# Setup joined to the batch loop, with the first two batches' head-0 scores taken from small fp32 products

## The reference

```python
x = L0_attn_x                                  # (B=8, T=512, C=128)
xn = layernorm(x)
x = x + attn(xn) + ffn(xn)

# attn: 16 heads of 8; q, k, v = split(xn @ w_attn.T + b_attn)
att = q @ k.T / sqrt(8), causal
S = relu(att[:, 0]); S[..., 0] = 0; S[diagonal] = 0
FF = cumsum(S shifted down by one row, axis=1)
att = att - FF[:, None]                        # for all 16 heads
keep = rank of FF in its row < min(101, i + 1), or the diagonal
y = softmax(where(keep, att, -inf)) @ v
attn = y @ w_proj.T + b_proj

# ffn: gates softmax(xn @ gate_w.T + gate_b), top 2 of 8 experts
inter_e = xn @ wi.T + bi + (xn @ lora_A[e].T) @ lora_B[e].T
ffn = sum over chosen e of (top_1 + top_2) * (relu(inter_e) @ wo.T + bo)
```

## Time and profile before

| | |
|---|---|
| median of 3 runs | 795.98 us (793.61 to 798.28) |
| the profiled execution | 799.05 us |
| its span, first to last instruction | 797.1 us |
| mean granted TensorE clock | 0.933 |
| busy: TensorE, VectorE, ScalarE, GpSimd | 592.1, 549.3, 378.2, 435.4 us |

### The profile page before, as it was taken

The page is one execution under the profiler, slowest core; times in us unless marked ns, Lnnn a source line. Parts: engine busy times, 40 slices in busy tenths (PEclk is TensorE's granted clock), DMA queues, the critical chain, the costliest instruction groups (busy, mean ns, idle before and its releaser), DMA issues. The chain is left out here.

```text
span 797.1 us, 16830 instructions
## 1 busy us (share of the span) xinstructions
PE 592.1 (74%) x5478; PEld 400.7 (50%) x5478; DVE 549.3 (69%) x2257; ACT 378.2 (47%) x806; POOL 435.4 (55%) x739
## 2 busy tenths in 40 slices
PE   4233029888788888878987878878888788879995
PEld 2111026465555564556645654547546664656574
DVE  6746416599748984699669964798459864897352
ACT  4124105564546554564556454645455454635443
POOL 4322226546845584547754684557564684439542
PEclk9998559999999999999999999998999899989998
DMA  3511130002500051003200250005100240000000
GB/s 83 66 14 25 26 53 5 1 2 38 71 1 2 14 72 23 1 1 58 50 1 1 36 73 1 2 1 71 23 2 2 43 53 1 1 11 6 1 2 14
DMA packets 27287, 18.98 MB, mean 24 GB/s; under 512 B 5418, under 2 KB 27073, under 8 KB 27201
## 3 DMA queue, kind: packets, MB, share of 16 engines
q1 hardware_dynamic: 27200, 17.91, 15.2%
HBM read 3.22 MB, written 2.10 MB: 7 GB/s over the span
## 5 line engine op out<-in xcount | busy, mean ns | idle before, releaser
L506 POOL TENSOR_SCALAR ar<-ar,mx 128x512 f32<-128x512 f32 (+3 forms) x512 | 280.2, 559 | 242.8 <-DVE mx L1156 242.0
L1156 DVE CUSTOM_DVE_ANT_0 ar<-ps_s,mask 128x512 f32<-128x512 f32 (+3 forms) x512 | 231.1, 485 | 77.3 <-PE ps_s L798 74.5
L809 PE MATMUL ps_t<-ident,ar 128*128 128x128 f32 x1280 | 210.0, 284 | 40.4 <-ACT pr L657 24.2
L657 ACT ACTIVATE pr<-ps_t 128x512 f32<-128x512 f32 (+1 forms) x352 | 191.0, 554 | 95.5 <-PE ps_t L809 94.9
L809 PEld LDWEIGHTS ps_t<-ident,ar 128*128 128x128 f32 x1280 | 158.3, 145 | 82.9 <-POOL ar L506 63.4
L798 PE MATMUL ps_s<-ks,qs 96*128 96x512 bf16 (+3 forms) x512 | 133.2, 314 | 41.6 <-PEq L1195 38.1
L825 PE MATMUL ps_o<-pr,va 128*32 128x128 f32 x2560 | 103.3, 292 | 18.9 <-ACT out_t L666 11.3
L798 PEld LDWEIGHTS ps_s<-ks,qs 96*128 96x128 bf16 x512 | 44.3, 102 | 92.2 <-issue 69.8
L825 PEld LDWEIGHTS ps_o<-pr,va 128*32 128x32 f32 x2560 | 66.4, 114 | 47.2 <-ACT pr L657 29.5
L642 ACT ACTIVATE h<-ps_m,bi_col 128x512 f32<-128x512 f32 x64 | 43.8, 685 | 83.4 <-PE ps_m L756 83.4
L756 PE MATMUL ps_m<-zm,b_t 128*128 128x512 f32 x128 | 70.0, 629 | 5.7 <-ACT h L642 5.4
(11 more groups left out here) (172 smaller groups left out, 801.9 us busy)
## 6 DMA issues: line engine op xcount, KB each, us to landing
qs<-parts SPq DMA_DIRECT2D x48, 128.0 KB
ks<-parts SPq DMA_DIRECT2D x48, 128.0 KB
xs<-in_L_attn_x SPq DMA_DIRECT2D x8, 256.0 KB, 3.3
out<-res SPq DMA_DIRECT2D x8, 192.0 KB, 2.1
out<-res SPq DMA_DIRECT2D x8, 64.0 KB, 6.4
ar<-in_L_ffn_wi SPq DMA_DIRECT2D x1, 256.0 KB
ar<-in_L_ffn_wo SPq DMA_DIRECT2D x1, 256.0 KB
ar<-in_L_ffn_lora_B SPq DMA_DIRECT2D x4, 64.0 KB
```

The lines of the kernel that those rows point to most:

```text
L506: nc.gpsimd.tensor_scalar(col, col, -1.0, mx[:, t % NA_RING, j:j + 1], ALU.mult, ALU.add)\
L657: nc.scalar.activation(pr[:, u % NP_RING, 0:w], ps_t[u % NT_RING][:, 0:w], ACT.Exp, scale=-1.0)\
L809: last = nc.tensor.transpose(ps_t[u % NT_RING][:, P * j:P * j + P], ar[:, u % NA_RING, P * j:P * j + P], ident[:, :])
L1156: nc.vector.tensor_tensor_reduce(out=ar[:, t % NA_RING, w * j:w * j + w], in0=ps_s[t % NS_RING][:, w * j:w * j + w], in1=mask[:, k % 2, OF ...
```

## The change

The two blocks become one. The slots of the setup are numbered from -26 (`AHEAD`) to -1 and run straight into slot 0.

- SP issues x, the attention weights, the eight small weights, the second x, and then the large feed-forward weights. Each job waits for its own weights.
- In the setup the side jobs rotate over all eight PSUM banks.
- Batch 0's and batch 1's head-0 scores no longer read the stacks. Two fp32 products of depth 128 with 8 output rows (`q0`, `k0`) give q and k of head 0 alone, and `s0` to `s3` are fp32 products of depth 8 from these (`head0`, which borrows the tiles `res` and `down`). Other batches take the stacks as before.
- Batch 1's moments, norm and transposed input stay in the setup; its q, k, parts, stacks and routing move into the first slots of batch 0 (`SECOND_AT`).
- The memsets of stack 0 are now one ahead of the moments and one behind them on VectorE; those of stack 1 come right behind the first root on GpSimd. `bqk_dh` is made by ScalarE.
- The split of the output biases (`bias_parts`) runs on VectorE at slot 9 of batch 0, and its transfer is waited for by GpSimd's first sum of hidden layers (`w_rows`).
- For all later batches scores, scans, reads and search of head 0 start two slots later (`s0` 13 to 15, `scan0` 14 to 16, `f0` 18 to 20, `search` 22 to 24, `under` 30 to 32, `reach` 31 to 33), while `marks` and what follows stay. `z` moves from slot 1 to 5, `mask0` and `mask1` from 3 and 4 to 7 and 8.
- x has three buffers instead of four, `ar` seven slots instead of six.

```diff
-XN = 4
+XN = 3
-NA_RING, NP_RING = 6, 6
+NA_RING, NP_RING = 7, 6
-FFN_JOBS = [("z", 1, "act"), ("mask0", 3, "dve"), ("mask1", 4, "dve")] + \
+FFN_JOBS = [("z", 5, "act"), ("mask0", 7, "dve"), ("mask1", 8, "dve")] + \
...
+AHEAD = 26
+FIRST_AT = {
+    "moments": 0, "root": 0, "norm": 1, "xt": 2, "q": 9, "k": 9,
+    "rest_q": 9, "second_q": 10, "third_q": 13, "rest_k": 9, "second_k": 11, "third_k": 13,
+    "s0": 5, "s1": 6, "s2": 7, "s3": 8, "scan0": 6, "scan1": 7, "scan2": 8, "scan3": 9,
+    "f0": 9, "f1": 10, "f2": 11, "f3": 12,
+    "gate": 14, "route": 16, "choices": 21, "share": 24,
+    "search": 13,
...
+    "flag": 24, "mask_0": 24, "mask_1": 24, "mask_2": 24, "mask_3": 24, "v": 25,
+}
+SECOND_AT = {
+    "moments": 3 - AHEAD, "root": 3 - AHEAD, "norm": 21 - AHEAD, "xt": 22 - AHEAD, "q": -1, "k": 0,
+    "rest_q": 0, "second_q": 1, "third_q": 2, "rest_k": 1, "second_k": 2, "third_k": 3,
+    "gate": 2, "route": 4, "choices": 6, "share": 7,
+}
...
+HEAD_JOBS = [("q0", 0, 3 - AHEAD), ("k0", 0, 3 - AHEAD), ("q0", 1, 23 - AHEAD), ("k0", 1, 23 - AHEAD)]
+WEIGHT_JOBS = [("w_attn", 0), ("small", 9), ("rows", 9), ("w_in", 20), ("w_out", 20), ("lora_b", 20)]
+BIAS_AT = 9
...
+        head0 = [tile[0:HD, :, :].rearrange("d a c -> d (a c)") for tile in (res, down)]
...
+                        elif name in ("q0", "k0"):
+                            wait_read(pe, "xt", n)
+                            wait_read(pe, "w_attn", 0)
+                            heads = (wq if name == "q0" else wk)[:, :].rearrange("c (d h) -> c d h", d=HD)
+                            last = nc.tensor.matmul(m[0:HD, :], heads[:, :, 0], xnt[:, c, :], start=True, stop=True)
...
                             j = int(name[1])
-                            if nth(n) >= 0:
-                                pe.wait_ge(stacked, 192 * (nth(n) + 1))
+                            if n <= 1:
+                                wait_read(pe, "k0", n)
+                                last = nc.tensor.matmul(m[:, 0:T - P * j], head0[1][:, P * j:P * j + P],
+                                                        head0[0][:, P * j:T], start=True, stop=True)
+                            else:
+                                pe.wait_ge(stacked, 192 * (n + 1))
...
+                                    if f == 0:
+                                        if k >= 1:
+                                            wait_full(pool, "down1", k - 1)
+                                        else:
+                                            pool.wait_ge(w_rows, 32)
...
-                    for t in range(end):
+                    for t in range(-AHEAD, end):
...
-        run_block(0, 1, setup=True)
-        run_block(STEPS, STEPS - 1)
+        run_block()
```

More of the change, by code:

```diff
@@ L112, with __init__ @@
     [(f"s{c}", "act") for c in range(NA)] + [(f"f{a}", "dve") for a in range(NA)] + [("flag", "dve")]
[L114 to L119, removed]
+NW, NW_SMALL = 6, 8
+HEAD_JOBS = [("q0", 0, 3 - AHEAD), ("k0", 0, 3 - AHEAD), ("q0", 1, 23 - AHEAD), ("k0", 1, 23 - AHEAD)]
+WEIGHT_JOBS = [("w_attn", 0), ("small", 9), ("rows", 9), ("w_in", 20), ("w_out", 20), ("lora_b", 20)]
+BIAS_AT = 9
 class Plan:
[L125 to L130, removed]
+    def __init__(self):
+        jobs = [(o - AHEAD, (name, 0), "act") for name, o in WEIGHT_JOBS]
+        jobs += [(t, (name, m), "act") for name, m, t in HEAD_JOBS]
+        for k in range(B):
             jobs += [(NU * k + o, (name, k), who) for name, o, who in FFN_JOBS + ATT_JOBS]
-        jobs += [(self.slot(name, n), (name, n), who) for name, who in PREP_JOBS
-                 for n in (self.early if name in EARLY else self.late)]
+        jobs += [(self.slot(name, m), (name, m), who) for name, who in PREP_JOBS for m in range(B)]
         jobs.sort(key=lambda x: x[0])
-        self.at, self.number, self.place, self.reads, self.last = {}, {}, {}, {}, []
+        self.at, self.number, self.bank, self.before, self.reads = {}, {}, {}, {}, {}
+        self.last = {}
         counts = {"act": 0, "dve": 0}
+        early, now, pair = 0, 1, None
         for i, (t, key, who) in enumerate(jobs):
@@ L140, in __init__, with slot @@
             if key[0][0] == "h" and key[0][2] == "1":
-                self.place[key] = self.place[key[0][:2] + "0", key[1]]
-                self.last[self.place[key]] = key
-            else:
-                self.place[key] = len(self.last)
-                self.last.append(key)
+                bank, pair = self.bank[key[0][:2] + "0", key[1]], None
+            elif pair is not None:
+                bank = 1 - pair
+            elif t < 0:
+                bank, early = early % NBANKS, early + 1
+            else:
+                bank = 1 - now
+            if t >= 0:
+                now = bank
+            if key[0][0] == "h" and key[0][2] == "0":
+                pair = bank
+            self.bank[key] = bank
+            self.before[key] = self.last.get(bank)
+            self.last[bank] = key
+            if bank >= NM_RING:
+                assert t < 0
             counts[who] += 1
             self.reads[key] = (who, counts[who])
[L150 to L156, removed]
+    def slot(self, name, m):
+        if m == 0:
+            return FIRST_AT[name] - AHEAD
+        if m == 1 and name in SECOND_AT:
+            return SECOND_AT[name]
+        return PREP_AT[name] + NU * (m - 1)
 def build(nc, x, w_attn, b_attn, w_proj, b_proj, wi, bi, wo, bo, lora_a, lora_b, gate_w, gate_b, out):
@@ L386, in make_stacks @@
                             stack, part = ((qs, Q_PART), (ks, K_PART))[t]
                             for j in range(len(part)):
-                                sp.dma_start(stack[8 * j:8 * j + 8, into(n), :, :], parts[:, t, part[j], :])\
-                                    .then_inc(stacked, 16)
-                    fetch(1)
-                    if setup:
-                        make_stacks(0)
-                        sp.wait_ge(w_prep, 3)
-                        for j in range(2):
-                            sp.dma_start(bias_rows[0:3, j, :, :], bias_part[:, j, :, :, :]).then_inc(w_rows, 16)
-                        sp.wait_ge(w_rows, 32)
@@ L398, in _ @@
-                    for k in range(steps):
-                        if k in plan.early:
-                            make_stacks(k)
+                                sp.dma_start(stack[8 * j:8 * j + 8, into(m), :, :],
+                                             parts[:, t, part[j], :]).then_inc(stacked, 16)
+                    fetch(0)
+                    sp.dma_start(raw_attn, w_attn.rearrange("(t p) c -> p t c", p=P)).then_inc(w_first, 16)
+                    sp.dma_start(raw_bqk[:, :], b_attn[0:2 * P].rearrange("(t p) -> t p", p=P)).then_inc(w_first, 16)
@@ L445, in pool_prepares @@
                     def pool_prepares(n, t):
-                        if setup and n == 0 and t == at("third_k", 0) + 1:
+                        if n == 1 and t == at("root", 0):
                             for stack in (qs, ks):
@@ L658, in _ @@
                                 .then_inc(weighed, 1)
-                        for kk in range(steps):
+                        for kk in range(B):
                             for a in range(NA):
@@ L785, in fill, with wait_early @@
                         last.then_inc(m_full, 1)
+                    def wait_early(bank):
+                        for i, one in enumerate(banks):
+                            if one is bank and i in plan.last:
+                                wait_read(pe, *plan.last[i])
                     def score(u):
```

380 lines of the change are left out of this document (201 added, 179 removed), and 8 rows, old and new, of tables (FIRST_AT, PREP_AT).

## The result

The kernel with the change took 750.46 us, the median of 4 runs (746.2 to 753.04), against 796.45 for the kernel before (4 runs, 793.61 to 798.28): a ratio of 0.9422 with a 95% interval of 0.9381 to 0.9462. The forecast was 750.6. The profiled execution took 753.04 with a span of 751.2, 45.9 less than the span of before.

A forecast was written before the change was run, and what follows sets the result against it. Bound: a long setup (first loop score at 114.04 us), then TensorE and VectorE by turns within batches. Lead 42.9 after batch 0 plus 2.5 later makes 45.4, off 799.05 profiled: 753.7, or 750.6 for the median; range 736 to 765.

The forecast's parts named there:

- The front of the setup: Setup up to the loop's first score: without stacks for head 0, that score comes at 60.2 instead of 114.04, 53.8 us earlier.
- What comes back in batch 0: Batch 0: GpSimd, late until 75.1, cuts the lead to 47.4 us; another 4.5 behind it leaves 42.9.
- the split biases: VectorE at slot 9 of batch 0: 3.5 to 7.2 us there, 0 to 5 on the path, 1.9 taken.
- the price of the later search: Stretch between search start and its unchanged end slot: VectorE's loses two units, TensorE's gains two, +1.8 us per batch, seven batches.
- the eight such waits: Slot 9 of batch 0: VectorE's bias split waits for GpSimd shifts of some 0.46 us, adding at most 3.7 us.
- The rows' wait: GpSimd's first sum, slot 16 of batch 0, waits for the bias rows' transfer: 0.5 us taken, bounds 0 and 6.
- the late bound: Upper bound of 6 us for the bias rows' wait; called the likely landing if rows queue behind the stack transfers.
- Later batches: Loop after batch 0: 5.3 us of stack waits saved, 2.8 lost net over seven batches, so 2.5 less in all.
- z's move: Later batches: z and its two masked products leave VectorE's full stretch for slots 5 to 8, -1.4 us per batch.
- Nothing comes back: Rival, chance 0.14: the lead of 53.8 us stays through batch 0 and later batches give 8, so 734 us.
- The long setup: Rival, chance 0.22: GpSimd's memsets lengthen the setup by 7.0 us or batch 0 loses 5.5 more: 763.1, up to 778.
- The exact selection: Rival, chance 0.02: a row's count leaves its bounds, thirteen exact rounds run once, 52 us more: 802.6 us.

The follow-up runs named there:

- bias_setup: Changed kernel with the split of the output biases made in the setup, ahead of the first scan, instead of at slot 9 of batch 0: 747.77 us, ratio 0.939.
- z_early_rows: Changed kernel with early z and masked products after batch 0, biases split in the setup, bias rows issued between both batches' stacks: 738.02 us, ratio 0.93.
- both_old: Changed kernel with both slot moves undone for later batches (head-0 scores to search, and z with its masked products): 758.13 us, ratio 0.9525.
- z_early: Changed kernel with z back at slot 1 and its masked products at 3 and 4 in batches 1 to 7: 743.29 us, ratio 0.9335.
- stacks0: Changed kernel with batch 0's head-0 scores waiting for the stacks again and 34 setup slots instead of 26: 777.55 us, ratio 0.975.
- large_first: Changed kernel with the large weights' loads issued ahead of the small ones again, as in the kernel before: 747.2 us, ratio 0.9414.

## Why the forecast was right, and where only its sum was

*The front of the setup: right.* The four small products took 4.6 us from 16.0, where 5.1 were summed; the search began 2.1 earlier than forecast (30.2 against 32.3), and the last mask was complete at 62.3, not 63.7. The first score came 0.8 later than forecast (60.97 against 60.2), and this closeness is partly luck: the stacks were issued 2.1 us earlier than forecast (31.35 against 33.5) and took 29.6 us from issue to first use and not 26.7, longer than the 27 that the prediction names as a sign of being wrong. The stack alone set the first score: the first mask was there 2.7 us earlier, at 58.3. The fp32 row was the one to take for the small products in this execution; in others they took 2.4 us in all, nearer to the bf16 bound of 1.5 (last section).

*What comes back in batch 0: GpSimd right in its end, the rest short by 3.6.* GpSimd came free at 75.0 as summed, but it began its shifts 1.4 us earlier than forecast and waited 0.48 and 1.16 us for VectorE between them, where the prediction had no gap. Its lead was then 47.5 (47.4 forecast). The forecast takes 4.5 from that; the runs show 8.2, in three parts:

- Up to slot 14 the lead falls 4.9 us (to 42.6), where 0.8 for the masked products and 1.9 for the split biases were summed. The biases are mis-sized: with them in the setup the kernel is 3.8 us ahead at slots 10 to 12 and 4.6 at slot 14, so their whole length reached the path.
- From slot 14 to 30 it falls 1.4 (1.3 and 0.5 were summed).
- From slot 30 to 34 it falls 1.9, and nothing was summed. This is the price of the later search. I charged it to "seven batches" only; batch 0 prepares a batch too, its search is moved as well, and it has no late stack of before to win against.

The split took 4.0 us on VectorE (3.5 forecast), its conversions 0.49, 0.28 and 0.28, nothing like the 8.02 of the earlier trace rows. That is not because GpSimd's shifts are short. GpSimd had almost nothing to do there: it ended a shift at 81.87 and then waited 3.63 us for VectorE. The one conversion that began beside a shift (81.52) is the one that took 0.49. By the rule of the Trainium skill (SBUF — State Buffer, Who interferes with whom) that VectorE's copies or casts in a two-port mode and GpSimd exclude each other, this one would have been held up; the trace agrees as far as one conversion goes, and the eight such waits that I had counted had nothing to wait for. In bias_setup a conversion at 18.14 beside a GpSimd instruction of 1.01 us took 0.28, so there no hold-up is seen.

The rows' wait was 0.44 us (0.5 forecast), but only because the unit before was late: with the biases early it was 6.09, the late bound. The transfer did stand behind batch 1's stacks, and issued ahead of them in z_early_rows it made nobody wait. The runs don't tell whether SyncE's order alone did that or also the choice of DMA engines by which I had weighed the late bound.

*Later batches: the sum of 2.5 was 6.3, by terms that were wrong.* The price of the later search was right: 1.9 us per batch between slots 30 and 34, where 1.8 was summed. The late stacks were mis-sized. I had counted half their "mean of 2.1", 5.3 in all; without the shift they would have cost this kernel more, 22.0 us in six waits with early z, and the lower clock behind each wait on top. The whole shift of slots, summed as a loss (12.6 - 5.3 = 7.3 us), is a gain of 14.8 there (both_old against z_early). And z's move has the wrong sign: "-1.4" per batch or 9.8 in all, because it left VectorE's full stretch, but it costs 7 (4.5 by the ratios; z_early against the changed kernel). I had asked which engine is fuller on the mean and not who stands in line for the product. The two errors, 22 and 17 us, have opposite signs, so their sum was off by only 5: both together give 7.6 us (758.1 to 750.5), 6.3 by the lead. Batch 0's error of 3.6 took back most of the rest. So the closeness of 750.6 is luck: two of its terms are off by 22 and 17 us and cancel.

The prediction's own signs say the same. Batch 0 took 13.8 us more than before from its first score to its store, not 7 to 11, and by their first masked scores later batches moved by up to 3.4 us (batch 6 from 86.9 to 83.5), not by less than 1.

*The rivals.* "Nothing comes back" fell with the 13.8 us lost in batch 0. The long setup fell with the first score at 61. The exact selection did not run: no instruction of its lines is in the trace. The change did what it says, as stacks0 shows.

## What to carry to other kernels

When a product gets a new slot, ask which in-order readers will stand in front of it and what queues behind them; the engine's share of busy time in that stretch doesn't say. When a schedule is moved for all batches, charge the move also to the one whose stall it doesn't cure. And when the cure of one wait makes a later step early, look whether its transfer is still queued behind something slow: here the early biases kept 2.2 of their 3.8 to 6 us in a profiled execution while the rows waited behind the stacks, and 7 to 8 us were there once the queue's order was changed with them. And when a forecast comes true, check its terms: here two large ones were wrong and cancelled.

## What the runs showed of the hardware

The same fp32 products in the same place take one of two durations in different executions. In the changed kernel the product of 512 columns (two passes) at 16.02 took 2.07; in large_first, whose work until then is the same on TensorE:

```profile
16.04 1.12 PE L773 MATMUL ps_o<-res,down 8*128 8x512 f32 x2 [0.77 <-ACT down L549]
17.00 1.46 PE L773 MATMUL ps_s<-res,down 8*128 8x384 f32 x6
18.39 0.33 PE L734 MATMUL ps_m<-ident,ar 128*128 128x128 f32 x1
...
19.31 2.06 PE L755 MATMUL ps_t<-xnt,wq 128*128 128x512 f32 x2
```
